# Spreading a recurrence's value rows by DMA copies and a GpSimd product, in a four-layer kernel on one core

## The reference

```python
def step(s, inp):
    k_l, v_l, w_l, r_l = inp
    a = k_l[..., :, None] * v_l[..., None, :]
    out = jnp.einsum('bhs,bhst->bht', r_l, faaaa * a + s)
    s_new = a + w_l[..., None] * s
    return (s_new, out)
```

## Time and profile before

| | |
|---|---|
| time, median of 3 (range) | 1263.58 us (1258.09 to 1264.42) |
| the profiled execution: its time, its span | 1264.44 us, 1262.5 us |
| busy: PE, DVE, ACT, POOL | 1127.0, 956.6, 651.5, 261.0 us |
| one steady turn | 143.4 us |
| mean granted TensorE clock | 0.945 |

### The profile page before, as it was taken

How to read it: one execution, slowest core, us unless ns; L and a number is a source line. 1 busy time by engine, 2 the same in 40 slices (tenths; PEclk the granted TensorE clock), 3 DMA queues, 4 the chain that set the end, 5 groups by cost and what they waited for, 6 DMA issues and landing times. The chain is left out here.

```text
span 1262.5 us, 24184 instructions
## 1 busy us (share of the span) xinstructions
PE 1127.0 (89%) x7776; PEld 765.1 (61%) x7776; DVE 956.6 (76%) x3401; ACT 651.5 (52%) x2483; POOL 261.0 (21%) x349
## 2 busy tenths in 40 slices
PE   5878899999999998999999998999999998897656
PEld 4564666665665666666666666666666666554434
DVE  2707697789967998789968998689968998675834
ACT  1528343784448553774448553674438553582024
POOL 3210223102410214102420214102321214101310
PEclk9788899999999999999999999999999999898858
DMA  8000000000000000000000000000000000000000
GB/s 296 2 9 20 1 2 1 22 2 15 2 21 2 16 1 1 22 2 16 1 22 2 12 5 1 22 2 15 1 22 2 6 11 1 1 2 11 1 1 9
DMA packets 18092, 18.91 MB, mean 15 GB/s; under 512 B 7216, under 2 KB 16432, under 8 KB 17712
## 3 DMA queue, kind: packets, MB, share of 16 engines
q1 hardware_dynamic: 17968, 17.37, 4.6%
HBM read 15.27 MB, written 2.10 MB: 14 GB/s over the span
## 5 line engine op out<-in xcount | busy, mean ns | idle before, releaser
L831 ACT ACTIVATE E<-S,nmax 128x128 f32<-128x128 f32 (+1 forms) x1024 | 424.1, 416 | 229.4 <-DVE nmax L1020 215.1
L1020 DVE CUSTOM_DVE_ANT_0 S<-psS,mb 128x128 f32<-128x128 f32 (+1 forms) x1024 | 264.3, 320 | 87.7 <-PE psS L534 64.4
L494 PE MATMUL ring<-slot,w_l 128*128 128x256 f32 x992 | 251.5, 400 | 14.0 <-DVE slot L1202 5.2
L494 PEld LDWEIGHTS ring<-slot,w_l 128*128 128x128 f32 x992 | 188.8, 198 | 60.0 <-issue 12.8
L548 PEld LDWEIGHTS psT<-ident,E 128*128 128x128 f32 x1280 | 146.2, 147 | 128.1 <-ACT E L831 73.3
L534 PE MATMUL psS<-keys,slot 32*128 32x512 f32 (+1 forms) x768 | 194.4, 581 | 30.1 <-DVE nmax L1020 19.0
L1035 DVE COPY ET<-psT 128x512 f32<-128x512 f32 x320 | 206.2, 681 | 7.8 <-PE psT L548 7.8
L548 PE MATMUL psT<-ident,E 128*128 128x128 f32 x1280 | 203.8, 293 | 7.8 <-DVE ET L1035 3.2
L831 ACT ACTIVATION_READ_ACCUMULATOR E<-S,nmax 128x1 f32 x1024 | 191.6, 187 | 0.0
L504 PE MATMUL ring<-w_l,slot 128*128 128x256 f32 (+1 forms) x640 | 151.9, 384 | 7.7 <-DVE slot L1051 5.8
L504 PEld LDWEIGHTS ring<-w_l,slot 128*128 128x128 f32 x640 | 115.3, 194 | 36.6 <-issue 10.7
(11 more groups left out here) (119 smaller groups left out, 1183.3 us busy)
## 6 DMA issues: line engine op xcount, KB each, us to landing
slot<-in_ctx SPq DMA_DIRECT2D x8, 256.0 KB, 2.7
slot<-in_x SPq DMA_DIRECT2D x8, 256.0 KB, 2.7
w_l<-in_wl SPq DMA_DIRECT2D x1, 2048.0 KB, 11.2
out<-slot SPq DMA_DIRECT2D x8, 256.0 KB, 2.1
w_l<-in_wl SPq DMA_DIRECT2D x2, 768.0 KB, 7.1
w_l<-in_wl SPq DMA_DIRECT2D x1, 1152.0 KB, 9.9
m0i<-in_m SPq DMA_DIRECT2D x8, 128.0 KB, 3.2
mb<-in_m SPq DMA_DIRECT2D x8, 128.0 KB, 2.8
```

What stands on the lines that cost most here:

```text
L494: m = pe.matmul(b[:, a, :], w[:, k, m0 + a * P:m0 + (a + 1) * P], src[:, k, :], start=(k == 0), stop=(k == kt - 1))
L831: ins = act.activation(E[:, g % RING_E, h * w:(h + 1) * w], S[:, g % RING_S, h * w:(h + 1) * w], ACT.Exp, bias=nmax[:, g % 4, h:h + 1], sc ...
L1020: ins = dve.tensor_tensor_reduce(S[:, g % RING_S, h * w:(h + 1) * w], psS[g % 2][:, h * w:(h + 1) * w], bias[:, bb, :], -1.0, HUGE, ALU.ad ...
```

## The change

The PE products that spread the value lanes are gone, with their matrix and their eight places in the ring of banks. In their place SP writes vT to a DRAM buffer v_rows, each channel row eight times (two transfers of 1024 rows of 1 KB), and reads it back in eight transfers of 256 KB, so that each state row has the value lane it needs in SBUF (VR, a ring of four). DVE's product kv moves to POOL (key_times_value, operands VR and kT, both in SBUF). DVE keeps the scans. The three orders are written anew.

```diff
+        VR = sb("VR", [RING_V, 2, T])
+        v_rows = nc.dram_tensor("v_rows", (P, 8, CT * T), F32, kind="Internal").ap()
+        v_spread = v_rows.rearrange("(c a h) i n -> c a (h i) n", c=4, a=2)
...
+                if 2 in streams:
+                    sp.wait_ge(leaves("v2"), left("v2"))
+                    for ct in range(CT):
+                        half = slice(ct * T, (ct + 1) * T)
+                        sp.dma_start(v_rows[:, :, half], vT[:, ct, :].unsqueeze(1).to_broadcast([P, 8, T]))\
+                            .then_inc(sems[f"v_out{ct}"], 16)
+                    for u in range(8):
+                        ct, j = u // 4, 2 * (u % 4)
+                        half = slice(ct * T, (ct + 1) * T)
+                        if j == 0:
+                            sp.wait_ge(sems[f"v_out{ct}"], turn(f"v_out{ct}"))
+                        if u >= RING_V:
+                            sp.wait_ge(sems["kv"], turn("kv", u - RING_V + 1))
+                        sp.dma_start(VR[:, u % RING_V, :, :],
+                                     v_spread[j % 4:j % 4 + 2, j // 4, :, half].rearrange("c p t -> p c t"))\
+                            .then_inc(sems[f"v_in{u % RING_V}"], 16)
...
-                def spread_v(u):
-
-                    ct, j = u // 4, 2 * (u % 4)
-                    b = start(f"vr{u}")
-                    for a in range(2):
-                        m = pe.matmul(b[:, a, :], spread_j[:, j + a, :], vT[:, ct, :], start=True, stop=True)
-                    m.then_inc(sems["product"], 1)
...
-                        dve.wait_ge(sems["product"], product(step))
-                        if u >= 2:
-                            dve.wait_ge(sems["scan"], turn("scan", u - 1))
                         dve.wait_ge(sems["seed"], turn("seed", u + 1))
-                        k_ = kT[:, ct, :].rearrange("p (b t) -> p b t", b=PAIR).unsqueeze(1)\
-                            .to_broadcast([P, 2, PAIR, P])
-                        dve.tensor_tensor(kv[:, u % 2, :, :, 1:P + 1],
-                                          bank(phase, step).rearrange("p a (b t) -> p a b t", b=PAIR), k_,
-                                          ALU.mult).then_inc(sems["emptied_D"], 1)
-                        dve.wait_ge(leaves(step), left(step))
+                        dve.wait_ge(sems["kv"], turn("kv", u + 1))
                         if u >= 2:
                             dve.wait_ge(sems["z"], turn("z", u - 1))
...
+                def key_times_value(u):
+
+                    ct = u // 4
+                    pool.wait_ge(sems[f"v_in{u % RING_V}"], turn(f"v_in{u % RING_V}", 16 * (u // RING_V + 1)))
+                    k_ = kT[:, ct, :].rearrange("p (b t) -> p b t", b=PAIR).unsqueeze(1).to_broadcast([P, 2, PAIR, P])
+                    pool.tensor_tensor(kv[:, u % 2, :, :, 1:P + 1],
+                                       VR[:, u % RING_V, :, :].rearrange("p a (b t) -> p a b t", b=PAIR), k_,
+                                       ALU.mult).then_inc(sems["kv"], 1)
```

More of the change, by code:

```diff
@@ L64 @@
 SCHEDULE = [
[L65 to L74, removed]
@@ new lines @@
+    7), "norm3", *jobs(0, 7, 8), "k2", "v2", *jobs(0, 8, 9), "d1", *jobs(0, 9, 10), "mr", "mg", *jobs(0, 10,
+    12), "r2", *jobs(0, 12, 15), "cols", *jobs(0, 15, 16), "inv0", "d2", *jobs(0, 16, 18), "decay", "vr0",
+    "vr1", "sum0", "g2", *jobs(0, 18, 20), "vr2", ("gather", 0), "o0", "ruk", "vr3", "bonus", ("gather", 1),
+    "nT", "vr4", "hn", ("gather", 2), "apply0", "u0", "apply3", "u1", "u2", "vr5", ("gather", 3), "u3", "vr6",
+    "aT", ("gather", 4), "vr7", ("gather", 5), ("gather", 6), ("gather", 7), "yT", "yn", "m2", "x1T", "ynT",
@@ L88 @@
-    10, 12), "sum3", "o3"]
+    "o2", "norm4", "apply4", "xcT", "fk", "fr", "shift0", "fv", "x4T", "q3", *jobs(3, 0, 12), "inv3", "sum3",
+    "o3"]
 ENTRY = {"xT", "cT", "q0", "k0c", "k0l", "v0c", "v0l", "k1", "v1"}
@@ L117 @@
     xaT="A", t="A", mw="D", mk="D", mv="D", mr="D", mg="D", d1="A", d2="A", k2="A", v2="D", r2="A", g2="D",
-    bonus="D", yT="A", ynT="A", o2="D", xcT="A", fr="A", fk="A", fv="D", x4T="A", q3="A", sum3="A", o3="D",
-    **{f"vr{u}": "D" for u in range(8)})
+    bonus="D", yT="A", ynT="A", o2="D", xcT="A", fr="A", fk="A", fv="D", x4T="A", q3="A", sum3="A", o3="D")
 PRODUCTS = {p: [s for s in steps_of(p) if s in EMPTIES] for p in PHASES}
 EMPTIED = {p: {e: [s for s in PRODUCTS[p] if EMPTIES[s] == e] for e in "AD"} for p in PHASES}
-assert len(PRODUCTS["steady"]) == len(EMPTIES) and len(EMPTIES) % BANKS == 0
+assert len(PRODUCTS["steady"]) == len(EMPTIES)
 IN_ORDER = {"start": [], "first": [0, 1], "steady": [0, 1, 3], "closing": [0, 1, 3], "last": [3]}
@@ L167 @@
     mask_bias0=(0, 2, 0), mask_bias3=(0, 0, 1), m3_in=(0, 0, 16), s0_in=(0, 0, 32), out_done=(0, 0, 16),
-    xf=(0, 0, 5), seed=(0, 0, 8), scan=(0, 0, 8), z=(0, 0, 8), gathered=(0, 0, 8), first_token=(0, 0, 2),
+    xf=(0, 0, 5), seed=(0, 0, 8), scan=(0, 0, 8), kv=(0, 0, 8), z=(0, 0, 8),
+    **{f"v_out{ct}": (0, 0, 16) for ct in range(CT)}, **{f"v_in{r}": (0, 0, 16 * (8 // RING_V)) for r in range(RING_V)}, gathered=(0, 0, 8), first_token=(0, 0, 2),
     shift=(0, 0, 2),
@@ L361, in counts, with bank @@
             return turn, before, product, left
-        def bank(phase, name):
-            made_before = ahead_of(phase, "product") + PRODUCTS[phase].index(name)
+        def bank(phase, i, name):
+            made_before = counts(phase, i)[2](name) - 1
             return ring[made_before % BANKS][:, :].rearrange("p (a b) -> p a b", a=2)
@@ L965, in _ @@
                             head8[:, :].unsqueeze(1).to_broadcast([P, 8, 16]))
-            for j in range(8):
-                at = lane_at(j)
-                dve.tensor_copy(spread_j[:, j, :].rearrange("p (a b) -> p a b", b=8),
-                                ident[:, at:at + 16].unsqueeze(2).to_broadcast([P, 16, 8]))
             for half in range(2):
@@ L1148, in program @@
                         dve.wait_ge(sems["product"], product("m2"))
-                        dve.tensor_tensor(X1, bank(phase, "m2"), XB2, ALU.add).then_inc(sems["emptied_D"], 1)
+                        dve.tensor_tensor(X1, bank(phase, i, "m2"), XB2, ALU.add).then_inc(sems["emptied_D"], 1)
                     elif step == "v1":
@@ L1167, in program @@
                         dve.wait_ge(sems["product"], product("o1"))
-                        dve.tensor_tensor(Y1, bank(phase, "o1"), XB1, ALU.add).then_inc(sems["emptied_D"], 1)
+                        dve.tensor_tensor(Y1, bank(phase, i, "o1"), XB1, ALU.add).then_inc(sems["emptied_D"], 1)
                     elif step == "norm1":
```

85 lines of the change are left out of this document (44 added, 41 removed).

## The result

The changed kernel takes 1327.0 us (median of 4 runs, 1326.1 to 1327.8) against 1261.4 us before: ratio 1.052, 95% interval 1.049 to 1.056. It is slower. The forecast was 1316 us with a range of 1260 to 1345.

What follows compares the result with a forecast made beforehand. PE, busy 89%, was taken to set the turn's length, with the recurrence about as long before yT. 7 x (4.4 + 1.0) = +38 and last +15 gave +53 on 1264.4, 1317; forecast 1316 us, range 1260 to 1345.

Steps and rivals of the forecast that it cites:

- +53: Whole execution: six steady turns and closing +38 us, phase last +15, on 1264.4 us.
- Turns: Six steady turns and closing: each 4.4 us longer by the chain plus 1.0 by the clock, +38 us together.
- Chain: Recurrence up to yT: POOL's products delay yT, so a steady turn grows from 143.4 to 147.8 us, +4.4.
- six lie in the chain: 6 x 1.18 = 7.1 us: Steady turn's recurrence: six of POOL's kv products exclude the scans and add their full duration, 7.1 us (6.4 to 7.7).
- second rival: Steady turns: new order hides the chain, or it ends 3 us or more earlier; 1270 to 1285 us; chance 0.15.
- Clock: PE in each turn: a gap before yT may bring half clock, with m2 behind it; +1 us (0 to 3).
- Such a fall of 3 us: PE's clock after a gap before yT: a 3 us fall costs at most 1.5 us of work.
- PE's spreads: Stretch before yT: removing eight spreads frees 7.7 us of PE per turn, a gain only if yT comes earlier.
- The copies: v through memory: cost zero in steady turns; in phase last v's rows land about 9 us after v2's copy.
- Last: Phase last: +7 us for a later scan 0 and +8.3 up to Z 7's end, sum +15 (11 to 20).
- 7 x 1.18 = +8.3: Phase last, scan 0 to Z 7's end: all kv products but kv 0 add full duration to 20.2 us.
- first rival: Recurrence: the product excludes nothing, scans run beside kv, turn 138.1 us, total 1236 us; chance 0.10.

Runs made afterwards that it cites:

- e4: Changed kernel with GpSimd's product kv cut to 8 elements per partition, waits and copies kept: 1262.6 us, ratio 1.001.
- e3: Changed kernel with product kv back on DVE, both operands in SBUF, copies and new orders kept: 1316.6 us, ratio 1.043.
- e5: Changed kernel with idle PE products filling three of PE's gaps in each steady and closing turn: 1290.0 us, ratio 1.024.
- e6: Kernel before with 3 idle PE products in the 1.8 us gap at the turn's start: 1249.2 us, ratio 0.992.
- e8: Kernel before with one more, unused GpSimd product of kv's size, reading SBUF, behind each of eight seeds: 1320.4 us, ratio 1.047.
- e1: Changed kernel with the three orders of steps of the kernel before, copies and GpSimd product kept: 1309.7 us, ratio 1.038.
- e10: Changed kernel with its product cut to two columns of each block and the orders of the kernel before: 1254.0 us, ratio 0.994.
- e11: Kernel before with idle PE products in gaps of the steady turns and of phases first and last: 1233.9 us, ratio 0.977.
- e7: Kernel before with the added DMA copies of v alone, their rows read by no product: 1265.2 us, ratio 1.0035.
- e9: Kernel before with a GpSimd memset of 1300 elements, reading nothing, behind each of the eight seeds: 1290.1 us, ratio 1.023.
- e2: Kernel before with only the three new orders of steps, spreads on PE and product on DVE: 1321.0 us, ratio 1.047.
- e12: Changed kernel with the orders of the kernel before and idle PE products in its gaps: 1306.0 us, ratio 1.034.

## Why the prediction was right, and where its steps were off

**The total and the sign were right, and the mechanism is in part the one named.** +53 was forecast, the spans show +62.6. Without the product's bulk the loss is gone (e4); with an operand in PSUM instead of SBUF nothing of it exists (before); with the product on DVE from SBUF most of it is there (e3, +57 us). It is the SBUF product inside the recurrence, and what TensorE's clock makes of the gaps that it leaves. That the total came so close is in part luck: the terms of the turn are off in opposite directions.

**Turns: 7 x 5.4 = 38 forecast, +50.6 measured.** Over the six turns that can be compared it is 46.3 / 6 = 7.7 us per turn. After loses 5.5 us per turn to the clock (e5) where before lost 1.1 (e6), so the clock's part is +4.4. The rest, e5 against e6, is (871.2 - 851.3) / 6 = +3.3: chain and orders.

*Chain, forecast +4.4: over-sized.* The step that failed is "six lie in the chain: 6 x 1.18 = 7.1 us", set upon the old 22.7 us. Scan 0 to Z 7's end is 27.2 us, +4.5. Two things were missed. With next to no product anywhere (e4) the recurrence is 21.9, 0.8 less than before; DVE's kv, costed at nothing, is the likely reason, and was not isolated. And the six products add 5.3 us, 0.9 each, not 1.18; e8's eight add 1.0 each. With scan 0 at X + 1.9 (forecast 2.0) and 1.5 us from Z 7 to yT (forecast 1.8), yT is at X + 30.6 against the forecast's 33.6. Where the orders are the old ones the price is 6.2 us on the mean of six turns (e1 against e10), 1.0 each. So the second rival, that the new order hides the chain, was half true: it hid 3.9 us (e1 against after), and of the chain 1.4 us are left up to yT, 30.1 in e5 against before's 28.7.

*Clock, forecast +1.0 (0 to 3): under-sized.* It is +4.4 us per turn. The step that failed is "Such a fall of 3 us": the one fall was read from a stretch of 3 us, but in the turn shown each fall of the profile after lasts 6.8 or 6.9 us, and there are three: at the turn's start, before the bonus, and before yT. The turn from 750.3 has two, some 3.4 and 10.2 us long, and is the shortest, 147.4 us. My walk through the order gave PE some 16 us of waits before yT (10.6 measured) without asking how they would be cut up; the single wait of 5.06 us was not seen.

*The orders outside the recurrence.* In e5, at full clock, the stretch from yT to the turn's end is 80.2 us, where the forecast had 79.4 - 0.5 = 78.9. These 1.3 us were not forecast. Before X e5 takes 35.1 us, where before without its own fall takes 34.2 (e11, whose turn is 142.3). So 142.3 + 0.9 + 1.4 + 0.8 gives e5's turn of 145.4 back. Which instructions take the 0.9 and the 0.8 wasn't tried.

**PE's spreads, forecast to give nothing: right.** e10 has no spreads and next to no product; over its six turns yT comes between 1.4 us earlier and 1.0 us later than before.

**The copies: right.** kv 0 waits 0.41 us for its rows in a steady turn and starts 5.0 us before X; e7 shows the turns unchanged under them. In last v's rows arrive 10.2 us after v's copy ends (1231.38 against 1220.53 + 0.69); the forecast had 9.

**Last, forecast +15: measured +11.9.** The start was forecast at +7: scan 0 stands 33.1 us behind o3 against 28.3, +4.8, since the new order also has v copied 3.3 us earlier behind o3. From scan 0 to the end of Z 7 the forecast was 7 x 1.18 = +8.3, the same step that failed in the turns; it is 26.8 us against 20.2, +6.5. The Z to Z period is (1254.07 - 1237.34) / 5 = 3.35 us over the five periods that hold a kv, against 2.55 before and a forecast of 3.7; the two behind them hold none. By themselves the copies cost last 3 us (e7), and cutting the product gives back 10.2 (122.1 - 111.9, e4); the two add up to more than the whole, 12, so they overlap.

**The first rival, that the product excludes nothing, fell**, by the pair of scans of 3.32 us. An instruction that excludes nothing isn't free either: in the orders of before, e9's memsets still made the kernel 2.3% slower.

**Still open:** why after's falls of the clock last between 3.4 and 10.2 us and the one of before's turn about 3.5 (0.95 over 35.2 us before X); and which instructions of the two orders make up what e5 still has over e6, 46.6 us by the spans: 9.1 ahead of the first o3, 19.9 in the six turns, 17.6 in last (123.4 against 105.8).

## What to carry to other kernels

An operand's place can matter more than the engine that reads it. A product that took 0.67 us from PSUM and cost the chain almost nothing costs it about 1 us once both operands are in SBUF and GpSimd runs it, and on VectorE it still stretches the recurrence as long as GpSimd's products run beside it (1.66 us for the one that met a Z in e3). Relieving the busiest engine gives nothing if it then waits in longer pieces: price each new gap also by what the clock takes from the work behind it, and look for such gaps in the kernel as it is. Filling them with idle products made the kernel before 2.3% faster. And test an order on the work for which it was made: e2's +61 us come with a wait for a product that the changed kernel doesn't have.

## What the runs showed of the hardware that was not expected

- Idle products in gaps of 1.7 to 5 us hold the granted clock at 0.99 to 1.00 through a steady turn (e5), where without them it is at half for 20.5 us of the turn shown. That pays only where PE's own work is on the path: -37 us on the changed kernel, nothing per turn on e12.
- A SBUF-reading GpSimd instruction of 1.26 us lengthened the recurrence's period in last by 1.03 us (e8); a memset of 1.18 us left the scans at 1.28 us and the period at 2.53 (e9). A product from SBUF on DVE took 1.66 us beside a Z (e3), from PSUM 0.67.
- The copies raise what one queue moves from 17 to 51 MB in 1.26 ms, in packets of about 1 KB; in the steady turns every engine's busy time stayed as it was (e7).
